# A delta-rule attention block on one core: the block inversion on GpSimd cut into seven parts, and all engines reordered

## The chip, the cores and the metric

The kernel runs on 1 core of one Trainium2 chip. The metric is the device time of one execution in microseconds. Engines: TensorE (PE), VectorE (DVE), ScalarE (ACT), GpSimd (POOL) and SyncE (SP), which issues transfers.

## What is computed

Two sequences of 4096 tokens with 512 channels, in chunks of 128 tokens, float32. Cut to what matters here (the layer norm ahead, the fusion gate, the output norm and the feed-forward block that is added are left in words):

```python
q, k, v = (short_conv_silu(x @ W, cw) for W, cw in ...)      # 4 taps, causal
attn = -einsum('cd,ed->ce', kb, k) * strict_lower            # kb = beta * k, chunks
for i in range(1, chunk):                                    # forward substitution:
    attn[i, :i] += attn[i] @ attn[:, :i]                     # inverse of a unit lower triangle
attn = attn + eye
u, w = attn @ v, attn @ kb
# scan over chunks: u -= w @ S; o = q @ S + tril(q @ k.T) @ u; S += k.T @ u
ms = multiscale_conv(v)          # depthwise, causal, 3, 15 and 31 taps, then two products
o = w0 * ms + w1 * o + w2 * v    # softmax weights from x and three means of |.|
out = rmsnorm(o) @ Wo
ffn = sigmoid(xr @ Wr.T) * (relu(xk @ Wk.T) ** 2 @ Wv.T)     # xr, xk mix x with the token before
```

## The kernel before, in words

The work goes in NS = 32 steps of 128 tokens for both sequences (NB = 2) and four heads (H = 4). A loop over `i` runs NS + 2 times on every engine; in one pass it handles the front of step `i` (norm, transposes, first projections), the middle of step `i - 1` (convolutions, Gram matrices, inversion, feed-forward keys) and the end of step `i - 2` (state, channel mix, gate, output). In what follows `k` stands for `i - 1` and `c` for `i - 2`, as in the flags of the code. The order on each engine is written out by hand as a list of calls; engines wait for each other by semaphores, each named after the event it counts.

The parts around the change, with lines of the kernel before:

- TensorE: `project(s, pair)` (L501) makes two blocks of v (pairs 0, 1), k (2, 3) or q (4, 5) in the two `front` banks; a pair must wait until `copy_raw(s, pair - 2)` on ScalarE has emptied its bank (`raw_done`). `turn_x` (L488), `turn_tokens` (L530), `gram` (L538), `query_key` (L545), `key_state` (L615), `solve` (L622), `outputs` (L629), `ffn_key` (L647), `ffn_out` (L659), `kernel_mix` (L675), `turn_o` (L731, needs `normalize_o`), `attend` (L739).
- The inverse of each 128 x 128 unit lower triangle is built from 16 x 16 blocks. ScalarE scales the Gram matrices into `Bm` (`scale_B`, L972), SyncE writes them to memory (`write_rows`, L343) and reads the 64 diagonal blocks back, one on each of 64 partitions, as `Bu` (`read_rows`, L349). POOL inverts them column by column (`invert_units`, L426 to L432). SyncE writes `Xu` (L357) and reads it back as `Yq` (L366). Then TensorE doubles the block size three times: `inverse_W`, `inverse_Z` (L555, L566), `join_W`, `join_Z` (L575 to L589), `half_W`, `half_X` (L598, L606), with `mask_W`, `step_Y`, `turn_Y` on VectorE and `copy_W`, `spread_X`, `join_X`, `copy_half_W`, `join_half_X` on ScalarE in between.
- SyncE, behind `read_rows`, loads the next x (L321) and copies the block of x straight to out (`copy_x`, L327), 512 KB from memory to memory, to which POOL's `add_out` (L453) later adds.
- The long convolution: VectorE's `taps` (L1515), 169 operations a step, add tap after tap to `my`. Five taps' products a step come from ScalarE instead (`multiply_taps` into `prod`, L1106) and POOL issues a transfer that accumulates them in `my` (`add_taps`, L448). There is one `prod`: each `multiply_taps` waits until the accumulate before it has landed (`adds_before`). `first_taps` (L1095) sets `my` up.
- POOL also takes the powers: `deviation` (L399, L403), `norms_k` (L416), `norms_q` (L407, L411), `invert_o` (L439, L443), whose result `rro` is what `normalize_o` (L1203) on ScalarE scales by.

POOL's pass is, in order: `deviation(i)`, `add_taps(k, 2, 0)`, `add_taps(k, 3, 0)`, `invert_units(k)`, `add_taps(k, 3, 1)`, `invert_o(c, 0)` and `(c, 1)`, `add_taps(k, 3, 2)` and `(k, 3, 3)`, `add_out(c)`, `norms_k(k)`, `norms_q(k)`.

## Time and profile before

| | us |
|---|---|
| median of 3 runs | 3786.1 |
| lowest, highest | 3782.17, 3787.43 |
| the profiled execution | 3789.28 |
| its span, first to last instruction | 3787.5 |
| busy in the span: PE, DVE, ACT, POOL | 3383.6, 3165.3, 2761.4, 813.6 |

The page gives the busy time of each engine over the whole span. All numbers below count from the start of the span. Every step repeats the same instructions, so a stretch from one step's instruction to the same one of a later step, divided by the steps between, is one step. An idle time in brackets stands ahead of the instruction of its row, with what ended it.

### The profile page before, as it was taken

Reading aid. Unit: us, or ns where it says so; the run is one execution under the profiler, and the core shown is the slowest. Engines: PE = TensorE matmul, PEld = TensorE weight load, DVE = VectorE, ACT = ScalarE, POOL = GpSimd, SP = SyncE. Lnnn points to the kernel's source line nnn. Section 1 sums busy time; section 2 is a strip of 40 time slices with the busy share of each in tenths; the row PEclk is TensorE's granted clock in tenths of the full one; section 3 lists DMA queues with packets and bytes.
Section 4 is the critical chain, followed back from the end, with each engine's and each line's share of the span. In section 5 each row is a group of like instructions: output and inputs, shape, how many; then the busy total and the mean of one; then the engine's idle time right before and its main releaser. Section 6 shows DMA issues by size and latency. Waiting matters only on the chain.

```text
span 3787.5 us, 69932 instructions
## 1 busy us (share of the span) xinstructions
PE 3383.6 (89%) x22848; PEld 2490.8 (66%) x22848; DVE 3165.3 (84%) x7856; ACT 2761.4 (73%) x9144; POOL 813.6 (21%) x1457
## 2 busy tenths in 40 slices
PE   6898889989899988998999899889999888999877
PEld 5666667666676666676666676666766666766654
DVE  5988888888898888898888898888988888888884
ACT  5677777767777778786778777677777787777774
POOL 2022221122221222211222112222212222112220
PEclk8899999999999999999999999999999999999988
DMA  6012211122111222111222111221112221112210
GB/s 175 13 39 47 47 37 32 26 47 47 41 33 28 39 47 47 37 35 23 47 47 47 33 34 28 47 47 39 35 24 44 47 47 37 33 24 47 41 37 10
DMA packets 188307, 155.06 MB, mean 41 GB/s; under 512 B 111804, under 2 KB 145980, under 8 KB 187688
## 3 DMA queue, kind: packets, MB, share of 16 engines
q0 software_dynamic: 31744, 79.70, 12.3%
q1 hardware_dynamic: 156200, 70.89, 7.2%
q8 instruction: 182, 2.98, 0.3%
q14 instruction: 181, 1.48, 0.1%
HBM read 51.47 MB, written 52.95 MB: 28 GB/s over the span
## 4 chain that ended last, share of the span: by engine, by line
PE 48%; ACT 20%; DMA 12%; POOL 9%; issue 8%; DVE 2%; SPq 1%; ACTq 0%; POOLq 0%; DVEq 0%
PE dense L739 8%; PE dense L706 6%; PE dense L647 6%; PE dense L659 6%; PE dense L663 6%; POOL Xu L432 4%; POOL Tu L430 4%; PE front L501 3%; DMA my<-prod 3%; DMA rows_out<-Bm 3%; DMA units_out<-Xu 2%; DMA Bu<-rows_out 2%; PE small L675 2%; ACT my L1095 2%; ACT dense L1125 2%
## 5 line engine op out<-in xcount | busy, mean ns | idle before, releaser
L1515 DVE SCALAR_TENSOR_TENSOR my<-vT,mw,my 128x256 f32<-128x256 f32 x5408 | 2233.8, 483 | 52.4 <-DMA my<-prod 40.9
L706 PE MATMUL dense<-xsh,w 128*128 128x256 f32 x2048 | 483.7, 382 | 6.4 <-ACT xr L1157 6.3
L706 PEld LDWEIGHTS dense<-xsh,w 128*128 128x128 f32 x2048 | 369.5, 190 | 72.6 <-ACT xr L1157 13.4
L399 POOL TENSOR_SCALAR vare<-xsq 128x2 f32<-128x2 f32 x32 | 6.7, 210 | 1878.9 <-ACT xsh L845 1878.9
L448 POOL DMA_DIRECT2D my<-prod x160 | 142.7, 892 | 814.4 <-ACT prod L1106 434.3
L1106 ACT ACTIVATE prod<-vT,mw 128x256 f32<-128x256 f32 x480 | 208.8, 500 | 126.4 <-DMA my<-prod 123.8
L739 PE MATMUL dense<-wo,ms 128*128 128x512 f32 x512 | 288.9, 716 | 0.0
L501 PE MATMUL front<-xsh,wv 128*128 128x256 f32 x1024 | 231.9, 384 | 15.1 <-ACT xsh L860 15.1
L647 PE MATMUL dense<-xk,wfk 128*128 128x256 f32 x1024 | 241.0, 389 | 3.2 <-DVE xk L1491 3.2
L659 PE MATMUL dense<-wr,xr 128*128 128x512 f32 x512 | 233.6, 599 | 0.0
L501 PE MATMUL front<-xsh,wq 128*128 128x256 f32 x1024 | 231.9, 379 | 0.0
L663 PE MATMUL dense<-wfv,ka 128*128 128x512 f32 x512 | 230.2, 592 | 0.0
L501 PE MATMUL front<-xsh,wk 128*128 128x256 f32 x1024 | 226.7, 379 | 0.0
L684 PE MATMUL dense<-cm,ym 128*128 128x512 f32 x512 | 225.0, 592 | 0.0
L501 PEld LDWEIGHTS front<-xsh,wv 128*128 128x128 f32 x1024 | 192.8, 191 | 47.6 <-ACT xsh L860 20.3
L501 PEld LDWEIGHTS front<-xsh,wq 128*128 128x128 f32 x1024 | 192.0, 190 | 38.8 <-issue 14.8
L501 PEld LDWEIGHTS front<-xsh,wk 128*128 128x128 f32 x1024 | 194.0, 189 | 27.6
L647 PEld LDWEIGHTS dense<-xk,wfk 128*128 128x128 f32 x1024 | 191.3, 192 | 30.8 <-issue 3.4
L1453 DVE STREAM_TRANSPOSE Xq<-Yq 128x256 f32<-128x256 f32 x64 | 28.3, 442 | 218.7 <-DMA Yq<-units_out 218.7
L739 PEld LDWEIGHTS dense<-wo,ms 128*128 128x128 f32 x512 | 113.0, 233 | 126.4 <-issue 123.9
L675 PE MATMUL small<-my,km 128*128 128x256 f32 x768 | 194.0, 389 | 1.5 <-DVE my L1515 1.5
L1031 ACT ACTIVATE Bm<-cell,g 128x128 f32<-128x128 f32 x256 | 73.0, 368 | 166.0 <-PE cell L622 166.0
(181 smaller groups left out, 7062.2 us busy)
## 6 DMA issues: line engine op xcount, KB each, us to landing
my<-prod POOLq DMA_DIRECT2D x160, 384.0 KB, 4.4
xa<-in_x SPq DMA_DIRECT2D x32, 512.0 KB, 4.7
rows_out<-Bm SPq DMA_DIRECT2D x64, 256.0 KB, 3.5
out<-xb POOLq DMA_DIRECT2D x32, 512.0 KB, 6.1
Yq<-units_out SPq DMA_DIRECT2D x128, 32.0 KB, 2.0
w<-in_w SPq DMA_DIRECT2D x1, 2048.0 KB, 16.9
Bu<-rows_out SPq DMA_DIRECT2D x32, 64.0 KB, 3.0
units_out<-Xu SPq DMA_DIRECT2D x32, 64.0 KB, 3.4
```

The source lines that it names most:

```text
L430: then(e.tensor_tensor(Tu[:, 0:n, 0:j], Bu[:, j, j + 1:HQ][:, :, None].broadcast_to([UNITS, n, j]), Xu[:, j, 0:j][:, None, :].broadcast_to ...
L432: left = e.tensor_tensor(Xu[:, j + 1:HQ, 0:j], Xu[:, j + 1:HQ, 0:j], Tu[:, 0:n, 0:j], ALU.subtract)
L501: i = e.matmul(by_batch(front[pair % 2][:, c * W:(c + 1) * W]), wt[:, k, hs(c0 + c)], xsh[s % 2][:, k, :, 1:1 + P], start=(k == 0), stop=( ...
L647: i = e.matmul(dense[pair][:, c * W:(c + 1) * W], wfk[:, k, hs(2 * pair + c)], xk[:, k, :], start=(k == 0), stop=(k == CB - 1))
L659: i = e.matmul(dense[0][:, :], xr[:, k, hs(b)], wr[:, k, :], start=(k == 0), stop=(k == CB - 1))
L663: i = e.matmul(dense[1][:, :], ka[:, k, hs(b)], wfv[:, k, :], start=(k == 0), stop=(k == CB - 1))
L675: i = e.matmul(s_mix, km[:, p, :], my[h % 2][:, p, :], start=(p == 0), stop=(p == 2))
L684: i = e.matmul(dense[b][:, :], ym[:, k, hs(b)], cm[:, k, :], start=(k == 0), stop=(k == CB - 1))
L706: e.matmul(by_batch(o), w1[:, k, hs(2 * pair + c)], xsh[s % 2][:, k, :, 1:1 + P], start=(k == 0), stop=False)
L739: i = e.matmul(dense[b][:, :], ms[:, b, hs(h)], wo[:, h, :], start=(h == 0), stop=(h == H - 1))
L1106: i = e.activation(by_batch(prod[:, p, :]), vT[s % 2][:, c, :, off:off + P], ACT.Copy, scale=mw[:, col:col + 1])
L1515: i = e.scalar_tensor_tensor(o, vT[s % 2][:, c, :, off:off + P], mw[:, col:col + 1], o, ALU.mult, ALU.add)
```

## The change

What the work on POOL does:

- `invert_units(s, lo, hi)` now does columns `lo` to `hi - 1`, and POOL's list calls it seven times a step, with `add_taps`, `invert_o` between the parts.
- The block starts from zeros with ones on its diagonal (`clear_units`, ahead of the step's first accumulate, once the block of the step before has been written out). Column 0 is the negated column of `Bu`; every later column's product now covers `j + 1` columns instead of `j`. The transposed product with a mask of -1 (L426 before) and the mask in the constants go.
- `norms_k` and `norms_q` move from the end of POOL's pass to its beginning.

```diff
-            def invert_units(s):
...
-                then(e.tensor_tensor(Xu[:, :, :], Bu[:, :, :].rearrange("m j i -> m i j"), minus_lower, ALU.mult))
-                then(e.memset(Xu[:, :, :].rearrange("m i c -> m (i c)")[:, 0:HQ * HQ:HQ + 1], 1.0))
-                for j in range(1, HQ - 1):
+            def clear_units(s):
                 if s:
                     e.wait_ge(units_written, 16 * s)
+                e.memset(Xu[:, :, :], 0.0).then_inc(units_cleared.sem, 1)
+                e.wait_ge(*units_cleared.upto(s))
+                e.memset(Xu[:, :, :].rearrange("m i c -> m (i c)")[:, 0:HQ * HQ:HQ + 1], 1.0).then_inc(units_ready.sem, 1)
+            def invert_units(s, lo, hi):
+                if lo == 0:
+                    e.wait_ge(rows_read, 16 * (s + 1))
+                    e.wait_ge(*units_ready.upto(s))
+                    last_column[0] = unit_step.link(
+                        e.tensor_scalar(Xu[:, 1:HQ, 0], Bu[:, 0, 1:HQ], -1.0, None, ALU.mult))
+                for j in range(max(lo, 1), hi):
                     n = HQ - 1 - j
-                    then(e.tensor_tensor(Tu[:, 0:n, 0:j], Bu[:, j, j + 1:HQ][:, :, None].broadcast_to([UNITS, n, j]),
-                                         Xu[:, j, 0:j][:, None, :].broadcast_to([UNITS, n, j]), ALU.mult))
-                    left = e.tensor_tensor(Xu[:, j + 1:HQ, 0:j], Xu[:, j + 1:HQ, 0:j], Tu[:, 0:n, 0:j], ALU.subtract)
+                    e.wait_ge(*last_column[0])
+                    made = unit_step.link(
+                        e.tensor_tensor(Tu[:, 0:n, 0:j + 1], Bu[:, j, j + 1:HQ][:, :, None].broadcast_to([UNITS, n, j + 1]),
+                                        Xu[:, j, 0:j + 1][:, None, :].broadcast_to([UNITS, n, j + 1]), ALU.mult))
+                    e.wait_ge(*made)
+                    left = e.tensor_tensor(Xu[:, j + 1:HQ, 0:j + 1], Xu[:, j + 1:HQ, 0:j + 1], Tu[:, 0:n, 0:j + 1],
+                                           ALU.subtract)
...
                 if f:
                     deviation(i)
                 if k:
+                    norms_k(i - 1)
+                    clear_units(i - 1)
                     add_taps(i - 1, 2, 0)
+                    norms_q(i - 1)
                     add_taps(i - 1, 3, 0)
-                    invert_units(i - 1)
+                    invert_units(i - 1, 0, 3)
+                    invert_units(i - 1, 3, 5)
+                    invert_units(i - 1, 5, 7)
                     add_taps(i - 1, 3, 1)
                 if c:
                     invert_o(i - 2, 0)
                     invert_o(i - 2, 1)
                 if k:
+                    invert_units(i - 1, 7, 9)
                     add_taps(i - 1, 3, 2)
+                    invert_units(i - 1, 9, 11)
+                    invert_units(i - 1, 11, 13)
+                    invert_units(i - 1, 13, 15)
                     add_taps(i - 1, 3, 3)
```

The lists of TensorE, ScalarE and VectorE are written anew; SyncE's isn't changed. Two or three lines of each stand for them:

```diff
-                    project(i - 1, 4)
...
+                if f:
+                    project(i, 4)
...
-                    multiply_taps(i - 1, 3, 1)
...
+                    copy_raw(i, 2)
...
+                    step_Y(i - 2)
```

On ScalarE the stretch from weighing the parts of the output to its norm reads as follows before (`raw<-front` is `copy_raw`, `prod<-vT,mw` is `multiply_taps`, `y,so<-dl` is `square_o`, `vtok<-turn` and the row behind it are `copy_tokens`, `dl<-dl,rro` is `normalize_o`):

```order
L883 COPY raw<-front 128x2x128 x2
L1182 ACTIVATE ms<-ms,gw 128x128 x4
L1175 ACTIVATE y<-vtok,gw 128x128 x4
L883 COPY raw<-front 128x2x128 x2
L1106 ACTIVATE prod<-vT,mw 128x256 x3
L1197 ACTIVATE y,so<-dl 128x128 x8
L937 COPY vtok<-turn 128x512
L945 ACTIVATE turn,ft<-turn 128x128 x4
L1203 ACTIVATE dl<-dl,rro 128x128 x8
```

and now:

```order
L894 COPY raw<-front 128x2x128 x2
L1200 ACTIVATE dl<-dl,gw 128x128 x4
L1193 ACTIVATE ms<-ms,gw 128x128 x4
L887 COPY raw<-raw 128x4x3
L1186 ACTIVATE y<-vtok,gw 128x128 x4
L1117 ACTIVATE prod<-vT,mw 128x256 x3
L894 COPY raw<-front 128x2x128 x2
L1208 ACTIVATE y,so<-dl 128x128 x8
L894 COPY raw<-front 128x2x128 x2
L1214 ACTIVATE dl<-dl,rro 128x128 x4
```

The second `copy_raw` (pair 1) stood ahead of `multiply_taps(k, 3, 1)` and stands behind it; `copy_tokens(k, 2)` has left the stretch and `copy_raw(i, 2)` has come in.

Further up on ScalarE, from `first_taps(k, 2)` to `first_taps(k, 3)` (`my<-vT,mw`), with `normalize` (`xa<-`), `scale_B` (`Bm<-`), `copy_mix` (`ym<-`), `weigh_v` (`y<-vtok`) and `copy_xnT` (`xsh<-front`), it now reads:

```order
L862 ACTIVATE xa<-xa,nmr,rstd 128x512
L1106 ACTIVATE my<-vT,mw 128x256 x3
L983 ACTIVATE Bm<-cell,g 128x128 x8
L862 ACTIVATE xa<-xa,nmr,rstd 128x512
L1124 COPY ym<-small 128x256
L1186 ACTIVATE y<-vtok,gw 128x128 x4
L871 COPY xsh<-front 128x4x128 x2
L1117 ACTIVATE prod<-vT,mw 128x256 x3
L1106 ACTIVATE my<-vT,mw 128x256 x3
```

The first `normalize` stood behind `first_taps(k, 2)`, `weigh_v(c, 0)` behind `first_taps(k, 3)`, and of the two `copy_xnT` the second did too, where a halo copy stood in its place.

TensorE's list, from the first projections of a step to the second `join_W`, now reads (`front<-xsh,wv` and `wk` are `project` 0 to 3, `wq` of x8 is `project(i, 4)`, `dense<-cst,dl` is `turn_o`, `dense<-wo,ms` both `attend`, `dense<-xk,wfk` is `ffn_key`, `cell<-` the inverse's pieces):

```order
L516 MATMUL front<-xsh,wv 128x256 x16
L516 MATMUL front<-xsh,wk 128x256 x16
L746 MATMUL dense<-cst,dl 128x128 x4
L516 MATMUL front<-xsh,wq 128x256 x8
L746 MATMUL dense<-cst,dl 128x128 x4
L754 MATMUL dense<-wo,ms 128x512 x8
L662 MATMUL dense<-xk,wfk 128x256 x8
L570 MATMUL cell<-Yq,Bm 32x16 x32
L581 MATMUL cell<-Wq,Xq 32x16 x32
L662 MATMUL dense<-xk,wfk 128x256 x8
L590 MATMUL cell<-Yq,Bm 32x32 x16
L545 MATMUL turn<-cst,vT 128x128 x4
```

`inverse_W` stood right behind the first `turn_o`, and the pieces behind it had `turn_o`, `attend`, `attend`, `ffn_key`, `ffn_key` between them one by one; `turn_tokens(k, 2)` stood ahead of the projections and `turn_tokens(k, 3)` right behind them. The last pieces (`half_W`, `half_X`, `key_state(k, 0)`, both `solve`) now follow each other directly, and `kernel_mix(k, 2)` stands behind the last `solve`, not ahead of it. `turn_tokens(k, 2)` is now ahead of `turn_logits`.

## Rows read from the trace of the kernel before

**Rows 1.** Windows: length, PE, PEld, DVE, ACT, POOL busy, PEclk, DMA, GB/s.

```profile
184.66:3645.50 3460.84, 3158.83 (x21422) 2326.39 (x21420) 2955.86 (x7349) 2584.22 (x8573) 753.93 (x1349) 0.95 0.19 39
2862.50:2876.00 13.50, 7.70 (x141) 5.00 (x142) 6.35 (x17) 8.05 (x21) 3.67 (x6) 0.51 0.45 75
```

**Rows 2.** Waits of TensorE, whole span: total, times, longest, in us.

```profile
PE dense L731 <- ACT dl L1203: 117.6, 24, 12.6
PE turn L530 <- ACT turn L945: 101.8, 23, 21.0
PE cell L555 <- DMA Yq<-units_out: 66.1, 27, 12.1
```

**Rows 3.** Timeline of TensorE, one step: start, us, engine, line, operation.

```profile
2834.74 1.53 PE L675 MATMUL small<-my,km 128*128 128x256 f32 x6
...
2845.03 7.19 PE L501 MATMUL front<-xsh,wv 128*128 128x256 f32 x32 [0.26 <-ACT xsh L860]
2852.06 7.08 PE L501 MATMUL front<-xsh,wk 128*128 128x256 f32 x32
...
2865.60 1.11 PE L731 MATMUL dense<-cst,dl 128*128 128x128 f32 x4 [5.41 <-ACT dl L1203]
2868.88 1.05 PE L555 MATMUL cell<-Yq,Bm 32*32 32x16 f32 x64 [2.17 <-DMA Yq<-units_out]
...
2872.65 5.20 PE L739 MATMUL dense<-wo,ms 128*128 128x512 f32 x8
...
2878.41 3.70 PE L739 MATMUL dense<-wo,ms 128*128 128x512 f32 x8
...
2882.67 3.72 PE L647 MATMUL dense<-xk,wfk 128*128 128x256 f32 x16
...
2950.38 1.53 PE L675 MATMUL small<-my,km 128*128 128x256 f32 x6
```

**Rows 4.** Timeline of ScalarE, same step.

```profile
2836.31 1.31 ACT L1095 ACTIVATE my<-vT,mw 128x256 f32<-128x256 f32 x3 [0.50 <-PE small L675]
...
2838.22 2.14 ACT L972 ACTIVATE Bm<-cell,g 128x128 f32<-128x128 f32 x8
...
2843.22 1.29 ACT L1095 ACTIVATE my<-vT,mw 128x256 f32<-128x256 f32 x3
...
2864.27 2.54 ACT L1203 ACTIVATE dl<-dl,rro 128x128 f32<-128x128 f32 x8 [4.85 <-POOL rro L443]
```

**Rows 5.** Timeline of SyncE's issues, same step.

```profile
2845.35 0.69 SPq L327 DMA_DIRECT2D out<-in_x  x1
2861.85 0.61 SPq L357 DMA_DIRECT2D units_out<-Xu  x1
```

**Rows 6.** Timeline of POOL, same step.

```profile
2844.81 0.86 POOL L448 DMA_DIRECT2D my<-prod  x1 [5.97 <-ACT my L1095]
...
2848.94 0.12 POOL L427 MEMSET Xu<- 64x16 f32 x1
```

**Rows 7.** Line 448 from 2844.5 to 2845.2: that transfer's landing.

```profile
DMA to landing us min/median/max: 9.2/9.2/9.2
```

**Rows 8.** Timeline of SyncE's issues, the step at 1800.

```profile
1809.95 0.69 SPq L327 DMA_DIRECT2D out<-in_x  x1
```

**Rows 9.** Chain that ended last, in order of time, the step at 1800.

```profile
1809.99 15.59 DMA my<-prod
```

**Rows 10.** Timeline of SyncE's issues, the last step.

```profile
3652.02 0.67 SPq L327 DMA_DIRECT2D out<-in_x  x1
```

**Rows 11.** Timeline of POOL, the last step.

```profile
3652.68 0.85 POOL L448 DMA_DIRECT2D my<-prod  x1 [6.25 <-ACT my L1095]
```

**Rows 12.** Line 448 from 3652.4 to 3653: that transfer's landing.

```profile
DMA to landing us min/median/max: 13.9/13.9/13.9
```

**Rows 13.** DMA queues from 1821 to 1822: packets, MB, share of 16 engines.

```profile
q1 hardware_dynamic: 2, 0.13, 30.4%
```

**Rows 14.** Line 448, all 160 accumulate transfers.

```profile
DMA to landing us min/median/max: 3.9/4.4/15.8
```

More of the change, by code:

```diff
@@ L433, in invert_units @@
                     if j < HQ - 2:
-                        then(left)
-                left.then_inc(units_done.sem, 1)
+                        last_column[0] = unit_step.link(left)
+                    else:
+                        left.then_inc(units_done.sem, 1)
             def invert_o(s, b):
@@ L773, in tensor_program @@
                     logits(i - 2, 1)
+                if k:
+                    turn_tokens(i - 1, 2)
+                if c:
                     turn_logits(i - 2)
@@ L784, in tensor_program @@
                     query_key(i - 1, 1)
-                    kernel_mix(i - 1, 1)
                 if f:
@@ L788, in tensor_program @@
                 if k:
-                    turn_tokens(i - 1, 2)
+                    kernel_mix(i - 1, 1)
                     key_state(i - 1, 1)
@@ L1248, in scalar_program @@
                     copy_ms(i - 2, 0)
+                if k:
+                    first_taps(i - 1, 0)
+                if c:
                     copy_ms(i - 2, 1)
@@ L1288, in scalar_program @@
                     tanh_beta(i - 1)
-                    first_taps(i - 1, 2)
                 if f:
@@ L1292, in scalar_program @@
                 if k:
+                    first_taps(i - 1, 2)
                     scale_B(i - 1, 0)
@@ L1298, in scalar_program @@
                     copy_mix(i - 1, 0)
+                if c:
+                    weigh_v(i - 2, 0)
                 if f:
                     copy_xnT(i, 0)
-                    take_raw_halo(i, 1)
+                    copy_xnT(i, 1)
                 if k:
@@ L1323, in scalar_program @@
                     square_o(i - 2, 1)
-                if k:
-                    copy_tokens(i - 1, 2)
+                if f:
+                    copy_raw(i, 2)
                 if c:
                     normalize_o(i - 2, 0)
+                if k:
+                    multiply_taps(i - 1, 3, 2)
+                if c:
                     normalize_o(i - 2, 1)
@@ L1330, in scalar_program @@
                 if k:
-                    multiply_taps(i - 1, 3, 2)
+                    mix_half(i - 1)
                 if c:
                     copy_oT(i - 2, 1)
+                if f:
+                    take_raw_halo(i, 3)
+                    take_raw_halo(i, 4)
                 if k:
-                    mix_half(i - 1)
-                    copy_W(i - 1)
                     multiply_taps(i - 1, 3, 3)
-                    spread_X(i - 1)
+                    relu_key(i - 1, 0)
                 if f:
-                    take_raw_halo(i, 2)
-                    take_raw_halo(i, 3)
                     short_first(i, 0)
                 if k:
-                    join_X(i - 1)
-                    copy_half_W(i - 1)
-                    copy_tokens(i - 1, 3)
-                    relu_key(i - 1, 0)
-                    square_key(i - 1, 0)
-                if f:
-                    short_first(i, 1)
-                    copy_raw(i, 2)
+                    square_key(i - 1, 0)
+                    copy_tokens(i - 1, 2)
+                    relu_key(i - 1, 1)
+                    copy_W(i - 1)
+                    copy_mix(i - 1, 1)
+                    square_key(i - 1, 1)
+                    copy_tokens(i - 1, 3)
         def vector_program(e):
@@ L1635, in vector_program @@
+                    taps(i - 2, 3, 43, 44)
+                    taps(i - 2, 3, 48, 49)
+                    taps(i - 2, 3, 46, 47)
+                    taps(i - 2, 3, 51, 52)
+                    taps(i - 2, 3, 53, 55)
+                    taps(i - 2, 3, 49, 50)
+                    taps(i - 2, 3, 52, 53)
+                    taps(i - 2, 3, 56, 57)
+                    gate_value(i - 2, 0)
+                    taps(i - 2, 3, 57, 58)
                     taps(i - 2, 3, 55, 56)
-                    taps(i - 2, 3, 50, 51)
@@ L1710, in vector_program @@
                 if k:
+                    taps(i - 1, 1, 23, 24)
+                    taps(i - 1, 1, 16, 17)
+                    beta_half(i - 1)
+                    taps(i - 1, 1, 18, 19)
+                    gains(i - 1)
                     taps(i - 1, 1, 20, 21)
+                    taps(i - 1, 1, 22, 23)
+                    taps(i - 1, 1, 25, 26)
+                    taps(i - 1, 1, 24, 25)
+                    taps(i - 1, 1, 27, 28)
                 if c:
@@ L1794, in vector_program @@
                 if k:
-                    taps(i - 1, 2, 53, 54)
+                    taps(i - 1, 2, 36, 37)
+                    taps(i - 1, 2, 51, 52)
                 if c:
```

312 lines of the change are left out of this document (135 added, 177 removed).

## The prediction

> **What bounds the kernel now.** I read the windows first. From the second to the last full step one step takes 3460.84/30 = 115.4 us; TensorE is busy 105.3 us of it, VectorE 98.5, ScalarE 86.1 [rows 1]. So TensorE sets the pace, and VectorE is near enough to set it once TensorE gains ten. Then the waits of TensorE: it waits for the normalized output (`turn_o`), for the token squares (`turn_tokens`) and for the inverted units (`inverse_W`) [rows 2]: 285.5 us, 9 a step. I went through one step whose mark, the start of `kernel_mix(k, 0)`, is at 2834.74; times below with a + count from the mark. In that step the wait for `turn_o` is 5.41 us and the one for `inverse_W` 2.17 [rows 3]. Behind the first stands ScalarE, idle 4.85 us for POOL's power `rro` [rows 4]: POOL is in the unbroken block inversion and the power waits behind it. After the stall the granted clock is 0.51 for 13.5 us, in which TensorE is busy 7.7 us [rows 1]: the 1.2 GHz level. Four transposes take 1.11 us there; the eight matmuls of `attend` take 5.20 us, and 3.70 at the higher level [rows 3]. So about half of the 7.7 us is loss, 3 to 4 us a step.
>
> **What each part costs.** *The inversion.* 28 small operations remain, each up to 15 elements wider, the transposed mask product goes, a clearing of 256 columns comes. POOL is busy 753.93/30 = 25 us of 115 [rows 1], and the clearing and `norms_k` fall where it waits: nothing on the path either way. What matters is that `invert_o` now stands after 7 of 15 columns: its 5 us stall goes. The price is a later end of the inversion, because `add_taps` 1 and 2 now stand inside it and wait for ScalarE. `inverse_W` has been moved back behind `project(i, 4)`, both `attend` and `ffn_key(0)`, 14.4 us of TensorE work at 3.5 to 3.7 us a piece [rows 3]. It started 7.03 us after POOL had finished (`write_units` issued at 2861.85 [rows 5], `inverse_W` at 2868.88 [rows 3]).
>
> *The late transfer.* The other half of the change is what ScalarE and TensorE now do between +8 and +30. ScalarE's `multiply_taps(3, 1)` waits for the accumulate transfer of `add_taps(3, 0)`. Before, `copy_raw(i, 1)` stood ahead of it, so that `project(i, 3)` could go on; now it stands behind it. How late is that transfer? In the step read it is issued at 2844.81, 0.54 us ahead of SyncE's copy of x to out (2845.35), and lands after 9.2 us [rows 5 to 7]. Issued at 1809.99, with the copy at 1809.95, it takes 15.59 us [rows 8, 9]. With the copy 0.66 us ahead (3652.02 against 3652.68) it takes 13.9 [rows 10 to 12]: in both it lands 14.6 to 15.6 us after the copy's issue. Of the 32 such transfers ten take 13 us or more, eight of them with the copy issued before them or at most 0.12 us behind, two with it 0.3 behind; six take under 7, those with the copy 0.62 to 1.5 behind. While the transfer is out, two packets of the copy's queue that end in one microsecond are 0.13 MB together [rows 13]: the copy runs in pieces of 64 KB on a few engines, and the accumulate's last packets stand between them.
>
> The Trainium skill (DMA: Bandwidth & Descriptors, Queues, rings and completion order) says that a DMA engine serves its queues in turn, one whole packet at a time. By that rule a transfer that meets the running copy waits for its large pieces one by one, and the sum is the one below; were the engine shared by bytes, it would land after some 5 us and the step be the 107 us of the first rival. The rows that pair late landings with an early copy bear the rule out. The same page (SWDGE vs HWDGE vs iDMA) says that the descriptors of POOL's transfers are written by POOL's own cores, which would lay the late landing on the inversion behind it; that is part of the first rival.
>
> Which is first now? `normalize(i, 0)` moves ahead of `first_taps(2)`, 0.7 us, so that starts at +1.8 (now 2836.31, +1.57) and `scale_B` at +3.0 (now 2838.22, +3.48) [rows 4]. The copy follows `scale_B` by 7.13 us (2845.35 [rows 5]): +10.1. `first_taps(3)` now has `weigh_v(0)` (1.2) and the second `copy_xnT` (0.5) ahead of it: 3.0 + 2.0 (`scale_B`) + 0.7 + 0.25 + 1.2 + 1.0 + 1.2 (`multiply_taps`) = +9.3; the transfer goes out 1.59 us after that starts (2843.22 to 2844.81 [rows 4, 6]): +10.9. So the copy is 0.8 us **ahead** in every step, and the transfer lands at 10.1 + 14.6 = +24.7. The bounds for its time are 3.9 and 15.8 us, the shortest and longest of all accumulates [rows 14]; I take 13.8, by the 13.9 of the step with the copy 0.66 ahead, which it is nearest to.
>
> **The sum for one step.** TensorE: `project(i, 0)` starts at +8.7 (from +10.3, since `turn_tokens(2)` has gone ahead and one wait is saved) and three of the four pieces take 3.53 us each [rows 3]: +19.3. Then idle: landing +24.7, product 1.2, `copy_raw(i, 1)` 0.55: `project(i, 3)` at +26.5, 7.2 us of idle. Such an idle brings the lower clock, for 10 us or more; it now falls on this projection, 7.0 us instead of 3.5: +33.5. `invert_o` is over by then. `turn_o` 0.44, `project(i, 4)` 3.5, `turn_o` 0.44, `attend` 7.3, `ffn_key(0)` 3.65: +48.8. The units: product 1 at +25.9, `invert_o` until +30.2, two columns, the product and `add_taps(3, 2)` until +33, six columns of 0.9 us (fourteen took from 2849.1 to 2861.8 [rows 5, 6]), +39.4, and 7.0: +46.4. `inverse_W` doesn't wait. From the end of `ffn_key(0)` to the next mark was 2950.38 - 2882.67 - 3.65 = 64.1 us [rows 3]; without `project(k, 4)`, with the four small inversion pieces and two `turn_tokens`, 64.7. The order there has new gaps, since nothing stands between the pieces: `inverse_Z` 0.5 (VectorE's mask), `join_Z` 0.1, `half_X` 0.7, `key_state(0)` 0.65, the last `solve` 0.5, `kernel_mix(3)` 0.3 for VectorE's taps; 0.4 is saved before `turn_logits`: 67.1. In all **115.9 us**, against 115.4. VectorE waits some 7 us for `mix_half`, where it waited for the units: equal. Where the lower level lasts 13.5 us as in rows 1, another 1.7 is lost; I take 0.2 for it on average.
>
> 31 steps x 0.7 = 22 us. On the profiled execution (3789.3, 1.8 above its span) 3811; the median is 3.2 lower: **3808 us**. What this measurement can tell from no change is 0.2%, 7.6 us, which is 0.25 us a step.
>
> **Rivals.** *The transfer lands earlier (faster).* If `add_taps(3, 0)` goes out 0.3 us or more ahead of the copy, so if one of my two chains is off by 1.1 us together, it lands after 10.4: `project(i, 3)` starts 3.3 us earlier, and the units (+43.6) become the limit. 43.6 + 67.1 = 110.7 us, 31 x -4.7: 3640. If it lands after 5, no idle is left before `project(i, 3)` and a step is 107. For it: 22 of 32 were under 13 us. Against: both chains move the wrong way. The same end comes if it isn't the copy but the inversion behind the transfer that holds it up: only seven columns stand there now, done by +18.6, `project(i, 3)` would start at +20.4, and a step take 108 us, 3560. Against that: all 32 had the whole inversion behind them and took 4.7 to 15.8. Chance 0.2, of which 0.03 for the inversion. *The lower clock stays away (faster):* 3.5 us a step less, 3700. Every one of the 29 steady steps had it, with idles of 5 to 8 us: 0.08. *The end of the step grows (slower):* ScalarE now has `copy_tokens(3)`, `spread_X` and `join_X` ahead of `half_W`, and `scale_v` 2.4 us ahead of `copy_half_W`. I find `join_X` done 1.5 us before TensorE wants it. If ScalarE is later than that, each further us goes through `half_W`, `half_X` and `key_state` whole: 3 us late is +1.5 a step on top, 3855; chance 0.15, bounded by 3.5 us late, 3870. It speaks for it that VectorE and TensorE are both near their limit at this point, against it that ScalarE is idle a quarter of a step.
>
> **How the numbers follow.** The forecast, late transfer and gaps as sized, has 0.57, with a range of its own of 3755 to 3850, since the gaps (2.75 us) may be half or twice as large and the clock's loss 2 to 5 us: of this 0.17 fall below -0.2%, 0.09 within, 0.31 above. With the rivals: faster 0.2 + 0.08 + 0.17 = 0.45, same 0.09, slower 0.15 + 0.31 = 0.46. Both signs hold much, so the range reaches from the early transfer to the late ScalarE: 3640 to 3860.
>
> **What would show it.** In the profile after, TensorE's wait for `dl` by way of POOL's `rro` is gone, and a wait of `project` for `raw` of some 7 us a step stands at the top; ScalarE waits over 200 us in total for the accumulate transfer, and its longest landings are at the second transfer of each step, 13 us and more. Clock near 0.95 as now. Wrong: those landings at 5 to 10 us, or a step of 111 us.

## The result, and the profile after

| | before | after |
|---|---|---|
| median, us | 3786.8 | 3818.0 |
| lowest, highest | 3782.2, 3793.2 | 3809.8, 3821.1 |
| the profiled execution | 3789.3 | 3814.9 |
| busy: PE, DVE, ACT, POOL | 3383.6, 3165.3, 2761.4, 813.6 | 3381.8, 3159.1, 2760.3, 760.7 |

The changed kernel takes 1.0078 times as long, 95% interval 1.0055 to 1.0101 (four runs of each): slower by 0.8%. The work is the same; POOL's fell by 53 us, and the time went into waits. The waits of TensorE in the changed kernel (total, times, longest) answer to [rows 2]. `L746` is `turn_o`, `L516` is `project`, `L581` is `inverse_Z`, `L621` is `half_X`, `L630` is `key_state`:

```profile
PE front L516 <- ACT raw L894: 252.7, 28, 9.9
PE dense L746 <- ACT dl L1214: 42.0, 7, 18.1
PE cell L621 <- ACT YW L1027: 21.8, 32, 0.7
PE cell L630 <- ACT X L1032: 21.4, 32, 0.7
PE cell L581 <- DVE Wq L1476: 17.6, 32, 1.3
```

The three waits of [rows 2] are gone or small: 42.0 us for `turn_o`, 18.1 of it in one wait, 7.8 for `turn_tokens` and 0.5 for `inverse_W`. One of 9 us has come in 28 of the 32 steps, for `raw`, the bank that `project(i, 3)` needs. Who holds ScalarE, and with it VectorE, is in the rows of the costliest groups on the page of the profile (the last part of each row is the idle time ahead of the group, and what ended it):

```profile
L1117 ACT ACTIVATE prod<-vT,mw 128x256 f32<-128x256 f32 x480 | 210.6, 509 | 295.5 <-DMA my<-prod 295.4
L1507 DVE SCALAR_TENSOR_TENSOR xr<-xsh,rest,xr 128x256 f32<-128x256 f32 x128 | 53.7, 482 | 277.4 <-ACT xk L1072 277.4
```

Here is the chain in one step, whose mark is at 1336.98. TensorE:

```profile
1336.98 1.53 PE L690 MATMUL small<-my,km 128*128 128x256 f32 x6
...
1345.68 7.09 PE L516 MATMUL front<-xsh,wv 128*128 128x256 f32 x32
1352.61 3.62 PE L516 MATMUL front<-xsh,wk 128*128 128x256 f32 x16
1365.25 5.39 PE L516 MATMUL front<-xsh,wk 128*128 128x256 f32 x16 [9.02 <-ACT raw L894]
...
1381.69 3.62 PE L662 MATMUL dense<-xk,wfk 128*128 128x256 f32 x16
...
1453.09 1.53 PE L690 MATMUL small<-my,km 128*128 128x256 f32 x6
```

SyncE's copy of x to out in the same step:

```profile
1347.51 0.71 SPq L325 DMA_DIRECT2D out<-in_x  x1
```

POOL's accumulate transfer of `add_taps(3, 0)`:

```profile
1347.79 0.91 POOL L457 DMA_DIRECT2D my<-prod  x1 [4.45 <-ACT my L1106]
```

The landing of that transfer, by its line and a window around it:

```profile
DMA to landing us min/median/max: 15.6/15.6/15.6
```

And ScalarE's `multiply_taps(3, 1)`, with `copy_raw(i, 1)` right behind it:

```profile
1363.37 1.31 ACT L1117 ACTIVATE prod<-vT,mw 128x256 f32<-128x256 f32 x3 [9.40 <-DMA my<-prod]
1364.58 0.62 ACT L894 COPY raw<-front 128x256 f32<-128x256 f32 x2
```

The copy goes out 0.28 us ahead of the accumulate, which lands after 15.6 us. What the DMA engines do in the meantime is in the view of the queues from 1352.5 to 1361.5 (packets, MB, share of 16 engines; q1 has the copy, q0 the accumulate):

```profile
q1 hardware_dynamic: 6, 0.39, 10.1%
q0 software_dynamic: 6, 0.02, 1.1%
```

The copy's packets are 64 KB each and 2.4 us long. There are eight; the trace has them two at a time, one pair every 2.65 us, and between two pairs stand two packets of the accumulate, 3 KB each. By 1352.4, 4.6 us behind its issue, 112 of the accumulate's 128 packets are through; the last 16 are the ones that stand between and behind the large pieces. Of the 32 such transfers 28 land after 14.5 to 15.9 us, with the copy from 0.82 us ahead to 0.23 behind; the other four land after 4.4 to 6.8, and in these the copy follows 0.85 to 1.25 us behind. The windows show what the clock does meanwhile (length, PE, PEld, DVE, ACT, POOL busy, granted clock, DMA share, GB/s), first of 18 whole steps and then of two stretches around the idle time:

```profile
1340.25:3442.22 2101.97, 1894.28 (x12855) 1411.12 (x12854) 1769.87 (x4411) 1550.62 (x5149) 424.36 (x828) 0.94 0.19 38
```

```profile
1352.00:1358.00 6.00, 4.23 (x20) 3.37 (x18) 5.93 (x12) 1.97 (x8) 3.34 (x7) 1.00 0.12 47
1358.00:1360.00 2.00, 0.00 (x0) 0.00 (x0) 1.97 (x6) 0.00 (x0) 0.00 (x0) 0.60 0.17 69
...
1364.00:1366.00 2.00, 0.75 (x2) 0.66 (x3) 1.96 (x5) 2.00 (x11) 0.77 (x1) 0.50 0.00 0
1366.00:1368.00 2.00, 2.00 (x7) 1.55 (x6) 0.49 (x2) 2.00 (x14) 1.53 (x4) 0.50 0.74 138
1368.00:1370.00 2.00, 2.00 (x9) 1.75 (x8) 0.00 (x0) 2.00 (x7) 1.80 (x4) 0.84 0.33 58
1370.00:1372.00 2.00, 2.00 (x12) 1.74 (x12) 0.00 (x0) 2.00 (x7) 1.35 (x4) 1.00 0.03 8
```

A step takes 2101.97/18 = 116.8 us, against 115.4 [rows 1]. The granted clock falls to the 1.2 GHz level while TensorE stands idle and is back at 2.4 GHz before `project(i, 3)` is over: 5.39 us where 3.62 is the length at the higher level.

### The profile page after: what moved, and what is told of

Read it like the earlier page. It is cut to its first block, busy times and chain, and to the rows that moved or that the text cites. A ratio compares the mean times of both kernels' runs of the same rounds, so it can differ in the third digit from the quotient of the medians.

```text
span 3813.1 us, 69963 instructions
## 1 busy us (share of the span) xinstructions
PE 3381.8 (89%) x22848; PEld 2513.9 (66%) x22848; DVE 3159.1 (83%) x7856; ACT 2760.3 (72%) x9144; POOL 760.7 (20%) x1489
## 4 chain that ended last, share of the span: by engine, by line
PE 48%; ACT 23%; DMA 15%; issue 8%; DVE 4%; POOL 1%; ACTq 0%; POOLq 0%; DVEq 0%; SPq 0%
DMA my<-prod 14%; PE front L516 6%; PE dense L721 6%; PE dense L674 5%; PE dense L678 5%; PE dense L754 5%; PE dense L662 5%; ACT my L1106 3%; DVE my L1531 2%; PE cell L637 2%; PE small L690 2%; ACT dense L1136 2%; ACT prod L1117 2%; PE cell L644 2%; PE cell L645 1%
## 5 line engine op out<-in xcount | busy, mean ns | idle before, releaser
L516 PE MATMUL front<-xsh,wk 128*128 128x256 f32 x1024 | 291.0, 448 | 252.7 <-ACT raw L894 252.7
L516 PEld LDWEIGHTS front<-xsh,wk 128*128 128x128 f32 x1024 | 232.4, 230 | 306.1 <-ACT raw L894 264.1
L1507 DVE SCALAR_TENSOR_TENSOR xr<-xsh,rest,xr 128x256 f32<-128x256 f32 x128 | 53.7, 482 | 277.4 <-ACT xk L1072 277.4
L1079 ACT ACTIVATE ka<-dense 128x512 f32<-128x512 f32 x64 | 38.2, 597 | 314.7 <-PE dense L662 314.7
L662 PE MATMUL dense<-xk,wfk 128*128 128x256 f32 x1024 | 236.8, 385 | 12.0 <-DVE xk L1507 10.1
L516 PE MATMUL front<-xsh,wq 128*128 128x256 f32 x1024 | 232.8, 380 | 0.0
L516 PE MATMUL front<-xsh,wv 128*128 128x256 f32 x1024 | 229.6, 382 | 0.8 <-ACT xsh L871 0.8
L754 PE MATMUL dense<-wo,ms 128*128 128x512 f32 x512 | 229.4, 601 | 0.0
L516 PEld LDWEIGHTS front<-xsh,wq 128*128 128x128 f32 x1024 | 192.7, 191 | 39.1 <-issue 14.8
L516 PEld LDWEIGHTS front<-xsh,wv 128*128 128x128 f32 x1024 | 193.7, 192 | 27.6 <-issue 1.1
L678 PEld LDWEIGHTS dense<-wfv,ka 128*128 128x128 f32 x512 | 97.3, 190 | 122.4 <-issue 122.4
```

The source lines that it names most:

```text
L516: i = e.matmul(by_batch(front[pair % 2][:, c * W:(c + 1) * W]), wt[:, k, hs(c0 + c)], xsh[s % 2][:, k, :, 1:1 + P], start=(k == 0), stop=( ...
L662: i = e.matmul(dense[pair][:, c * W:(c + 1) * W], wfk[:, k, hs(2 * pair + c)], xk[:, k, :], start=(k == 0), stop=(k == CB - 1))
L678: i = e.matmul(dense[1][:, :], ka[:, k, hs(b)], wfv[:, k, :], start=(k == 0), stop=(k == CB - 1))
L754: i = e.matmul(dense[b][:, :], ms[:, b, hs(h)], wo[:, h, :], start=(h == 0), stop=(h == H - 1))
```

## The experiments

The theory after the result: the gap of a step is the late landing, the late landing is the copy that meets the transfer on the DMA engines, and POOL's inversion has no part in it. The rivals were the descriptors behind the inversion, the clock, and a limit elsewhere (ScalarE or VectorE) that would come back as soon as the wait went.

### The copy moved behind the reading of the units

```diff
-                    copy_x(i - 1)
...
                     read_units(i - 1)
+                    copy_x(i - 1)
```

This is the whole edit, on SyncE's list, once on the changed kernel and once on the kernel before. On the changed kernel:

> The changed kernel with one edit: SyncE issues its copy of x to out after the units have been read back (about 49 us behind the mark), not right behind the read of the rows. Theory (the copy's large pieces hold up the second accumulate transfer of a step): that transfer lands after 4 to 6 us in nearly every step, the wait of project(i, 3) for raw goes from 252.7 us in total to under 30, and a step takes 107 to 112 us like the three steps of the changed kernel whose transfer landed early: 3550 to 3680 us. Rival (it is the inversion behind the transfer, on POOL, that holds it up): landings stay at 15 us and the time at 3815. Second rival (the step has another limit just behind this one): landings short, but the time falls by under 1%.

Measured: 3522.6 us (3517.4 to 3524.3), 0.9299 times the kernel before, interval 0.9283 to 0.9315. The windows of 23 steps, with the same columns as above, read:

```profile
925.29:3385.79 2460.50, 2366.47 (x16423) 1749.20 (x16421) 2266.02 (x5634) 1976.19 (x6568) 576.30 (x1056) 0.99 0.21 42
```

All 160 accumulates land within 6.2 us (view of their line):

```profile
DMA to landing us min/median/max: 3.9/4.2/6.2
```

Two rows of TensorE's timeline show the place where the 9 us stood:

```profile
1364.68 7.08 PE L516 MATMUL front<-xsh,wk 128*128 128x256 f32 x32
1372.30 0.66 PE L746 MATMUL dense<-cst,dl 128*128 128x128 f32 x4 [0.54 <-ACT dl L1214]
```

A step takes 107.0 us, and `project(i, 2)` and `(i, 3)` run through in 7.08 us. That is 9.8 us a step less for one transfer that is issued some 26 us later. Seven columns of the inversion still stand right behind the second accumulate, as in the changed kernel, and it lands after 4.0 to 6.2 us: the theory that the inversion delays it has fallen. A version further down, with all fifteen columns right behind it and the copy as late, settles it: 4.0 to 6.5 us. The time came out below the 3550 that I had thought the least, though the step is the shortest that I had named: 31 steps of 9.8 us less are 304 us off 3818, which is 3514, so that bound was set too high. The clock over the whole execution rose to 0.981 from 0.936.

On the kernel before:

> The kernel before with the same edit, the copy issued after the units have been read back. Theory (before, TensorE waited for the power behind the unbroken inversion, whatever the transfer did): landings of the second transfer 4 to 6 us, time within 0.5% of 3787, since the steps with late landings (114.0 to 115.9 us) were no longer than the others. Rival (the copy cost the kernel before as much as the changed one): 3640 to 3700.

Measured: 3927.2 us (3921.7 to 3927.6), 1.0367 times, interval 1.0351 to 1.0382. This missed. There the copy goes out some 22 us behind the second accumulate and now meets the fourth. The landing of the one issued at 1417.94, with the copy issued at 1416.04:

```profile
DMA to landing us min/median/max: 12.9/12.9/12.9
```

and the waits (`L731` is `turn_o`, `L598` is `half_W`, `L1515` is `taps`):

```profile
PE dense L731 <- ACT dl L1203: 205.3, 32, 12.6
PE cell L598 <- ACT YW L1010: 72.6, 32, 3.7
DVE my L1515 <- DMA my<-prod: 170.5, 37, 8.9
```

What the collision raised are the last two: in the kernel before `taps` waits 40.9 us and `half_W` hardly at all. The wait for `turn_o` rose from 117.6 as well, but it is as long in the version below in which no accumulate meets the copy (199.8), so it is the inversion's and not the collision's. The second accumulate landed after 5 to 8 us as meant; the collision moved. The fourth lands after 12.0 to 13.3 us in all 32 steps, with the copy 1.7 to 2.8 us ahead of it. It costs wherever an accumulate is out that somebody waits for. So the kernel before had to be tried with the copy in a place where it meets nothing.

### The copy in small pieces

```diff
-                e.dma_start(out[:, s * P:(s + 1) * P, :], x[:, s * P:(s + 1) * P, :])...
+                e.dma_start(out[:, s * P:(s + 1) * P, :].rearrange("b p d -> p b d"),
+                            x[:, s * P:(s + 1) * P, :].rearrange("b p d -> p b d"))...
```

The changed kernel, with the copy at its old place and time and the same bytes, but the order of its dimensions turned, so that a piece is one token's 2 KB.

> The changed kernel with the copy of x where it was, but with both sides read as partition, batch, row, so that it moves in pieces of 2 KB spread over all DMA engines. Theory (what holds the accumulate up are the large pieces, not the 512 KB as such): second landing 5 to 8 us, wait of project(i, 3) under 60 us in total, time 3520 to 3620. Rival (any copy of this size beside it costs the same): landings above 12 us and 3800.

Measured: 3539.6 us (3525.9 to 3548.1), 0.9342 times, interval 0.9317 to 0.9368. The landings from 812 to 3421 us, 125 accumulates:

```profile
DMA to landing us min/median/max: 3.9/4.2/8.9
```

and TensorE's timeline of the pair (a line of the file further down):

```profile
1360.44 3.62 PE L517 MATMUL front<-xsh,wk 128*128 128x256 f32 x16
1364.27 3.73 PE L517 MATMUL front<-xsh,wk 128*128 128x256 f32 x16 [0.20 <-ACT raw L895]
```

So it isn't that two transfers overlap, nor how many bytes they move, but how the copy is cut. The edit changes two things at once: the pieces are 2 KB for 64, and they no longer move two at a time: the DMA engines are all busy from 1358.5 to 1361.5, at 267 GB/s, where the windows of the changed kernel give a share of 0.11 and 46 GB/s from 1352.5 to 1361.5. Small pieces that move on as few engines as the large ones weren't tried, so what each of the two is worth is open. The Trainium skill (DMA: Bandwidth & Descriptors, Queues, rings and completion order) has an engine serve its queues in turn, one whole packet at a time; this pair of runs agrees, 15.6 us against at most 8.9 for the same copy at the same moment, and so do the accumulate's packets that stand between the large ones in the changed kernel. The wait for `raw` is 22.2 us in all here, and it was 252.7.

### The wait moved, not removed

```diff
-                if k:
-                    multiply_taps(i - 1, 3, 1)
...
+                if k:
+                    multiply_taps(i - 1, 3, 1)
```

On ScalarE of the changed kernel, `copy_raw(i, 1)` goes ahead of `multiply_taps(k, 3, 1)` again, as in the kernel before.

> The changed kernel with copy_raw(i, 1) ahead of multiply_taps(k, 3, 1) on ScalarE again, as it stood in the kernel before. Theory: project(i, 3) no longer waits, but turn_o(0) does, since normalize_o(0) still stands behind the same product: landing +24.7, product 1.2, squares 2.4, copy 0.5, norm 1.2 give +30, so TensorE idles 7 us there; time 3800 to 3825. Rival (only the place of copy_raw costs): the wait goes and a step takes 109 us, 3600.

Measured: 3818.5 us (3814.8 to 3832.5), 1.009 times, interval 1.0067 to 1.0112: the changed kernel's own time. The wait went where `raw` had hidden it:

```profile
PE dense L746 <- ACT dl L1214: 315.3, 34, 22.4
```

The order of the two on ScalarE is worth nothing by itself: whatever stands behind the wait for the late transfer is late.

### The idle time filled

Two versions of the changed kernel in which TensorE repeats `project(i, 2)`, with the same result in the same bank: it is done three times in one, three and a half times in the other (6.9 and 8.7 us of added work a step).

```diff
-                for c in range(2):
+                for c in [c for _ in range(3 if s and pair == 2 else 1) for c in range(2)]:
```

> The changed kernel with the sixteen matmuls of project(i, 2) done three times over (same inputs, same bank, same result), which fills 7 us of TensorE's idle ahead of project(i, 3) with work. Theory (the idle costs a second time, by the lower clock over the projection that follows): the clock stays at the higher level there, project(i, 3) takes 3.5 us and not 7, and the time falls by 31 x 3.5 = 108 us to about 3705. Rival (the lower clock is hidden behind ScalarE and VectorE, which set the step's end): 3800 to 3840.

Measured: 3785.8 us (3779.2 to 3790.2), 0.9997 times, interval 0.9987 to 1.0007: 32 us under the changed kernel. The filler didn't reach far enough. TensorE's timeline, and the windows over it:

```profile
1117.48 10.55 PE L516 MATMUL front<-xsh,wk 128*128 128x256 f32 x48
1131.13 6.68 PE L516 MATMUL front<-xsh,wk 128*128 128x256 f32 x16 [3.10 <-ACT raw L894]
```

```profile
1129.00:1133.00 4.00, 1.87 (x5) 1.51 (x6) 3.93 (x10) 3.75 (x19) 1.47 (x3) 0.67 0.14 27
1133.00:1137.00 4.00, 4.00 (x11) 3.19 (x10) 0.00 (x1) 3.59 (x14) 3.28 (x7) 0.50 0.41 75
```

An idle time of 3.1 us was enough to bring the lower level, and now nearly the whole of it fell on work: 6.68 us for what takes 3.62. After an idle of 9.0 it was 5.39. So I filled further:

> The changed kernel, with seven half groups of project(i, 2) instead of two, so 8.7 us of repeated work where 9.0 us were idle (the first filling, 7 us, had left 3.1 us of idle behind it, and the clock fell in that). Theory (the lower clock costs the changed kernel what project(i, 3) takes longer, 5.4 us against 3.6): no fall of the clock there, project(i, 3) at 3.6 us, 28 steps x 1.8 = 50 us less than 3818, so about 3768. Rival (the fall costs nothing, later waits take it up): 3810 to 3820 or, where the filling overruns, more.

Measured: 3794.1 us (3783.7 to 3807.5), 1.0012 times, interval 0.9999 to 1.0026. Now the projection's matmuls (group of `wk` in the view of lines; mean in ns) are all at the higher level, and the clock is 0.975 over the execution:

```profile
L516 PE MATMUL front<-xsh,wk 128*128 128x256 f32 x2264 | 501.4, 380 | 9.6 <-ACT raw L894 9.2
```

In the changed kernel 1024 of them keep TensorE busy 291.0 us, 0.284 us each; here it is 501.4 us for 2264, 0.221 each, and over 32 a step the difference is 2.0 us. The filled kernel is 24 us under it, 0.8 us a step, where I had expected 50 us. So the lower clock over the projections cost the changed kernel between 0.8 and 2.0 us a step, not the 3.5 that I had charged. What became of the other 1.2 isn't settled. In part it went into new waits: `project(i, 3)` still waits 9.2 us for `raw` in all, and `turn_o` waits 30 times for ScalarE where it waited 7 times, 0.4 us in the step that starts at 1803.72. And the filler is in the way where the transfer lands early: two such steps take 112.7 us here, 110.9 and 112.1 in the changed kernel.

### The parts of the change by themselves

First the kernel before with the copy out of the way: SyncE waits for POOL's `norms_q`, the last work of its pass, before it issues the copy.

```diff
-                    copy_x(i - 1)
...
+                    e.wait_ge(*rq_done.upto(i - 1))
+                    copy_x(i - 1)
```

> The kernel before with the copy of x issued after POOL's norms_q, the last entry of its pass, so behind all five accumulates of the step. In the kernel before, the copy behind the read of the units had hit the fourth accumulate (13 us) and cost 3.7%. Theory (each accumulate that meets the copy lands late, and the kernel before is bound by the power behind the unbroken inversion once none does): all landings 4 to 7 us, a step 115 us, time within 1% of 3787. Rival (the kernel before gains as much as the changed one did from a copy out of the way, so that the new orders are worth nothing by themselves): 3520 to 3600.

Measured: 3776.8 us (3771.0 to 3780.9), 0.9973 times, interval 0.9961 to 0.9984. In the kernel before the collision was worth some 10 us, 6 to 15 by the interval; `turn_o` waits 199.8 us in all there for the power that stands behind the unbroken inversion. There the late transfer was hidden behind the stall that the inversion makes anyway. In the changed kernel the same collision was worth 295 us.

Then the kernel before with the cleared block and without the mask product, the inversion still unbroken (edit: the new `clear_units` and `invert_units`, called as `invert_units(i - 1, 0, 15)`):

> The kernel before with the block built from zeros and ones and without the mask product, the inversion unbroken and in its old place. Theory (POOL's own work is worth almost nothing, the mask product 1.1 to 2 us against 14 slightly wider columns): the units come 1 to 2 us sooner, and with them the power for which TensorE waits, so up to 1.5 us a step: 3740 to 3787. Rival (wider columns cost more than the product saved): 3790 to 3820.

Measured: 3760.3 us (3758.6 to 3765.0), 0.9932 times, interval 0.9915 to 0.9948. The transposed product, 2 us on POOL, is gone. Waits of TensorE for `turn_o` and for `inverse_W`, against 117.6 and 66.1 [rows 2]:

```profile
PE dense L744 <- ACT dl L1216: 122.3, 25, 12.6
...
PE cell L568 <- DMA Yq<-units_out: 55.7, 27, 11.1
```

`turn_o` waits as long in all as it did; `inverse_W`, and `turn_tokens` with 84.8 for 101.8, wait less.

Then POOL's seven parts and cleared block, with the copy out of the way, while the other engines keep the orders of before and `norms_k` and `norms_q` their place at the end of POOL's pass:

> The kernel before, its three other engines in their old orders and the copy behind norms_q, with POOL's seven parts and cleared block alone: invert_o after seven columns, add_taps 1 and 2 inside the inversion. Theory (the parts put the end of the inversion behind two accumulates, and the old TensorE order asks for the units right after turn_o(0)): turn_o waits less, but inverse_W waits some 12 to 17 us a step, time 3950 to 4200. Rival (the parts alone bring the gain, whatever the orders): 3600 to 3700.

Measured: 3939.0 us (3934.8 to 3940.1), 1.0402 times, interval 1.0387 to 1.0418. The wait for `turn_o` is down to 18.9 us; in its place the units come late, since parts of the inversion now stand behind accumulates that wait for ScalarE (628.9 us in all on POOL for `prod`, 416.3 in the version with the safe copy alone), and `inverse_W` (`L575` here) is still early on TensorE:

```profile
PE cell L575 <- DMA Yq<-units_out: 437.4, 32, 15.4
```

Last the other way round: all new orders, late copy, and the inversion in one piece at the place of its first part.

```diff
-                    invert_units(i - 1, 0, 3)
...
+                    invert_units(i - 1, 0, 15)
```

> The changed kernel with the late copy and the inversion unbroken in the place of its first part (fifteen columns ahead of the third accumulate), all else as in the changed kernel. Theory (the seven parts are worth the stall of invert_o): the power comes at about +29 and turn_o(0) waits from +23 to +30 in each step, with a fall of the clock: 7 to 9 us a step more than the 3522 of the late copy, so 3740 to 3800. Rival (the new orders on the other engines hide an unbroken inversion too): 3520 to 3580.

Measured: 4064.9 us (4059.7 to 4070.2), 1.0733 times, interval 1.0715 to 1.0751: 542 us, 17 us a step, over the same kernel with the parts. I had expected about half of it. Waits of TensorE (`L740` is `turn_o`, `L575` here is `inverse_Z`):

```profile
PE dense L740 <- ACT dl L1208: 263.4, 34, 21.4
PE cell L575 <- DVE Wq L1470: 248.5, 32, 9.8
```

There are two stalls, not one. The first is the known one for the power (ScalarE waits 229.4 us for `rro`). The second I hadn't seen: the later accumulates are held up behind the inversion, VectorE's `taps` wait 261.3 us for them, and `mask_W` stands behind those on VectorE. The copy is away here, and the second accumulate lands after 4.0 to 6.5 us with the whole inversion right behind it: the inversion holds up what POOL issues after it, not the transfer that is already out.

So neither half of the change is a gain alone, the parts (+4%) or the orders (+7%); together, with the copy away, they are worth 3776.8 - 3522.6 = 254 us. The move of `norms_k` and `norms_q` was never tried by itself; it is in the 254.

### Versions for the gaps

Of the gaps that the new order has brought I tried to close two, on top of the late copy: half of `ffn_key(1)` between `inverse_W` and `inverse_Z`, and the last quarter of `ffn_out`'s value terms between `half_W` and `half_X`.

```diff
+                    ffn_key(i - 1, 1, 0)
...
-                    ffn_key(i - 1, 1)
+                    ffn_key(i - 1, 1, 1)
...
-                    ffn_out(i - 1, 0)
+                    ffn_out(i - 1, 0, 0)
...
+                    ffn_out(i - 1, 0, 1)
```

> The changed kernel with the late copy, and two of the gaps on TensorE filled: the first half of ffn_key(1) between inverse_W and inverse_Z, the last of four terms of the value product between half_W and half_X. Theory (each of these waits, 19.8 and 21.8 us in the late copy's run, lies on TensorE's path): 3522 - 40 = 3480 to 3500. Rival (VectorE, busy 90% of the span there, sets the pace): 3515 to 3525.

Measured: 3551.1 us (3548.5 to 3554.8), 0.938 times, interval 0.9366 to 0.9394, 28 us over the late copy alone. `inverse_Z` became late for VectorE, which waits 48.3 us for it, and `solve` then waits 57.1 us for VectorE. With the second move alone:

> The late-copy kernel with one more move: the last value term of TensorE stands between half_W and half_X, so that the matmul behind the fourth part of the inversion finds its operand ready; inverse_W and inverse_Z stay where they are. Theory: the gap before half_X (21.8 us in all in the late-copy kernel) lies on the path, and the version with two moves lost its time by delaying inverse_Z past VectorE; then this one comes out 12 to 22 us under the late-copy kernel, 3500 to 3510 us. Rival: VectorE, 90% busy, sets the pace with TensorE, and the gap comes back behind it: 3518 to 3528 us.

Measured: 3506.0 us (3501.6 to 3511.3), 0.9257 times, interval 0.9236 to 0.9278; the best kernel of this study, 7.4% under the kernel before and 8.2% under the changed one. The time is the theory's, but its account isn't. The gap before `half_X` is gone and a new one stands before `solve`:

```profile
1403.77 1.16 PE L630 MATMUL cell<-S,kT 128*128 128x128 f32 x8 [0.67 <-ACT X L1036]
1404.77 1.06 PE L637 MATMUL cell<-y,X 128*128 128x128 f32 x8
1406.38 1.16 PE L637 MATMUL cell<-y,X 128*128 128x128 f32 x8 [0.56 <-DVE y L1490]
```

and the shortest steps are the same with and without the move: 105.4 us. Windows of single steps of the late copy alone, a short one behind a long one:

```profile
925.29:1034.67 109.38, 105.00 (x717) 77.86 (x716) 98.60 (x246) 86.04 (x287) 25.20 (x46) 0.97 0.20 41
1034.67:1140.10 105.43, 102.05 (x717) 75.34 (x716) 98.44 (x246) 86.07 (x287) 25.25 (x46) 1.00 0.21 42
```

In the long one `inverse_Z` waited 1.42 us for VectorE instead of 0.5, and the clock fell twice: `ffn_key(1)` right behind takes 5.41 us for 3.72, and `key_state(k, 0)` later on 2.08 us. Over 23 steps each the move took a step from 107.0 to 106.3 us: 5.6 of the 15.5 us are less busy time of TensorE, at a granted clock of 1.00 for 0.99, and 9.8 less idle time. The trace shows which falls of the clock the move took away. With the late copy alone `key_state(k, 0)`, which stands behind the idle times of 0.68 and 0.67 us for `half_X` and for itself, takes 1.3 to 2.1 us in 10 of the 32 steps and 1.16 in the others; with the value term in the first of these gaps it takes 1.16 in all 32. A fall right behind `inverse_Z` remains in six steps, and these take 107.3 to 111.2 us.

## Why the prediction was right, by its own steps

The forecast was 3808 us and the time is 3818; it was to be slower, and it is, by 0.8% where 0.6% was forecast. The direction was close to an even bet in the prediction itself, 0.46 for slower and 0.45 for faster; that it came out so is the late transfer, in which it was right. The step that starts at 1336.98, beside the sum (us from the mark):

| | forecast | measured |
|---|---|---|
| `project(i, 0)` starts | 8.7 | 8.7 |
| the copy is issued | 10.1 | 10.5 |
| the accumulate is issued | 10.9 | 10.8 |
| it lands | 24.7 | 26.4 |
| `project(i, 3)` starts | 26.5 | 28.3 |
| `project(i, 3)` ends | 33.5 | 33.7 |
| `ffn_key(0)` ends | 48.8 | 48.3 |
| from there to the next mark | 67.1 | 67.8 |
| the step | 115.9 | 116.1 |

**The inversion and `rro`.** Right. ScalarE waits for `rro` 10.7 us in 4 cases, where it waited 4.85 us in the step read [rows 4]. `inverse_W` doesn't wait.

**The late transfer.** Right in its mechanism, and both chains of issue times held within half a microsecond. Its size was off: I took 13.8 us by the step with the copy 0.66 us ahead [rows 10 to 12], and it is 15.6, as at 1809.99 [rows 8, 9], where the copy and the transfer go out together. The copy was 0.3 us ahead, not 0.8, and nearer to that row. Counted from the copy's issue it is 15.9 us, where the two rows had 14.6 and 15.6 and the sum took the lower. With an idle of 9.0 us for 7.2 this was 1.8 us a step too little. One reading was too neat: six transfers under 7 us had the copy 0.62 to 1.5 us behind, but three others with it 0.63 to 0.68 behind took 8.7 to 11.8.

**The clock.** The step that failed most. I had the lower level begin with the projection and charged 3.5 us. It began within the idle time (0.60 from 1358 to 1360) and was over before the projection was: 5.39 us for 3.62, 1.8 us. Both terms together are 10.8 us where the sum had 10.7; the forecast is as near as it is because the two errors are opposite, and that is luck. So is the next pair: from the end of `project(i, 3)` to that of `ffn_key(0)` it is 14.7 us for 15.3, `attend` taking 7.0 and not 7.3, and from there to the mark 0.7 us more. The price of the rival in which the clock stays up falls with it: the version with it up for the projections takes 3794, not 3700.

**The gaps.** `inverse_Z` 17.6, `half_X` 21.8 and `key_state` 21.4 us in all are 1.9 us a step, for which I had 1.85. The 0.9 us for `join_Z`, `solve` and `kernel_mix(3)` don't appear in the step read, but its end is 0.7 longer than the sum. What stands there is a second fall of the clock, which the sum had at nothing. A row of TensorE's timeline (`L630` is `key_state`) and a window over it:

```profile
1403.35 2.07 PE L630 MATMUL cell<-S,kT 128*128 128x128 f32 x8 [0.67 <-ACT X L1032]
1403.00:1405.00 2.00, 1.65 (x8) 1.66 (x8) 1.79 (x5) 0.29 (x1) 0.00 (x0) 0.50 0.00 0
```

`key_state(k, 0)` takes 1.16 us in four steps and 1.28 to 2.08 in the other 28. The kernel before, which has other work between these pieces, has no such fall there: its `key_state` never takes over 1.06. From the start of `key_state(k, 0)` to that of `kernel_mix(3)` it is 4.12 us in the step read and 3.09 in the step of the late copy from 1349.05, where the clock stays up: 1.0 us, by which the gaps cost more than their length. The last rival, ScalarE late at the end of the step, didn't occur: the waits of `half_X` and `key_state` are 0.7 at most.

**The first rival.** Its price was right. Landing after some 5 us, a step was to be 107 us, and with the copy moved it is 107.0. What it lacked was its condition in this kernel. The part of it that laid the late landing on the inversion has fallen with the same run and, with all fifteen columns behind the transfer, with the unbroken one.

**The share of short landings.** I had counted none; four of the 32 transfers landed early, and the steps from 181.58 and 643.28, which hold two of them, took 110.9 and 112.1 us. The other two stand at the two ends: the first step takes 124.3 us for 128.3 in the kernel before, and what follows the last mark 141.9 for 145.2. Against a step of 116.8 and not 115.9 elsewhere, these shorter stretches are why the profiled execution (3814.9) stands so near to the 3811 of the sum.

## What to carry to other kernels

A transfer that no engine is seen to wait for can still set the time: look at what is out on the DMA engines beside every transfer that is waited for, and at how it is cut into pieces, before any order is rewritten. Here one line moved on SyncE's list was worth 295 us, nearly ten times what the rewriting of four lists had lost. When work on one engine is cut up, its consumers have to be moved with it: parts without orders, and orders without parts, were each slower than the kernel before and the changed one. And a gap of under a microsecond between two short pieces has two prices, its length and, where it brings the lower clock, the work behind it.

## What the runs showed of the hardware

- A copy from memory to memory of 512 KB in two long rows, cut into eight packets of 64 KB that move two at a time, brings the landing of an accumulate of 384 KB on another queue from 4 to 6 us up to 14.5 to 15.9, if it is issued up to 0.8 us ahead of it or up to 0.23 behind, and to 12.0 to 13.3 if it is issued 1.7 to 2.8 us ahead. With the same copy in pieces of 2 KB, spread over the engines, the landing is at 8.9 us at most.
- Between two large packets the trace has one 3 KB packet of the other queue on each of the two streams: six and six from 1352.5 to 1361.5.
- POOL's columns behind an accumulate don't hold it up: 4.0 to 6.2 us with seven behind it, 4.0 to 6.5 with fifteen.
- Granted clock: an idle time of 3.1 us brought the 1.2 GHz level, and it then cost 3.1 us on the projection behind it; an idle time of 9.0 us brought the same level, and it cost 1.8, because most of it ran out while nothing was there to be slowed. A shorter idle time isn't a cheaper one in proportion.
- Idle times far shorter stand ahead of the lower level too. One of 1.42 us stands in a step whose granted clock is 0.97 and whose work on TensorE takes 105.0 us for 102.05. Two of 0.68 and 0.67 us with short pieces between them stand ahead of `key_state`, which then takes 1.3 to 2.1 us instead of 1.16 in 28 of 32 steps of the changed kernel and in 10 of the late copy; with the first of the two filled it takes 1.16 in all.
